# Spreading the keys of a banded attention over heads: by SBUF-to-SBUF DMAs instead of masked copies

## What is computed

```python
x = jnp.transpose(mask, (0, 2, 1))                 # the 256 columns are the positions, the 64 rows the features
q, k, v = jnp.split(x @ w_in.T + b_in, 3, axis=-1) # 8 heads of 8 features each
scores = jnp.einsum('bqhd,bkhd->bhqk', q, k) / jnp.sqrt(d)
band = jnp.abs(idx[:, None] - idx[None, :]) <= 64
scores = jnp.where(band[None, None], scores, neg)
attn = jax.nn.softmax(scores, axis=-1)
o = jnp.einsum('bhqk,bkhd->bqhd', attn, v).reshape(n, t, e)
```

## Time and profile before

| | us |
|---|---|
| median of 3 runs | 362.23 |
| lowest, highest | 362.06, 362.73 |
| profiled execution | 362.1 |
| its span, first to last instruction | 360.4 |

### The profile page before, as it was taken

How to read it: one execution, slowest core, us unless ns; L and a number is a source line. 1 busy time by engine, 2 the same in 40 slices (tenths; PEclk the granted TensorE clock), 3 DMA queues, 4 the chain that set the end, 5 groups by cost and what they waited for, 6 DMA issues and landing times.

```text
span 360.4 us, 7398 instructions
## 1 busy us (share of the span) xinstructions
PE 320.2 (89%) x2258; PEld 252.3 (70%) x2258; DVE 256.2 (71%) x935; ACT 208.1 (58%) x438; POOL 192.7 (53%) x287
## 2 busy tenths in 40 slices
PE   0689999779798898999999999899999999999993
PEld 0467768567576666767777777777777767888892
DVE  5899999999989899988323615576478846661364
ACT  2639888759687695967841341467577865213210
POOL 4757988758767585856602431515152543244733
PEclk9859999999999999999999999999999999999997
DMA  7996000000000000000000000000000000000011
GB/s 220 363 373 227 1 3 3 1 2 3 1 2 0 3 3 1 3 2 2 2 2 0 0 2 0 1 2 0 2 3 0 2 0 3 0 31 15 1 38 37
DMA packets 10150, 12.16 MB, mean 34 GB/s; under 512 B 1920, under 2 KB 8832, under 8 KB 10112
## 3 DMA queue, kind: packets, MB, share of 16 engines
q1 hardware_dynamic: 9536, 11.36, 9.2%
q10 hardware_dynamic: 576, 0.33, 0.4%
HBM read 10.64 MB, written 1.05 MB: 32 GB/s over the span
## 4 chain that ended last, share of the span: by engine, by line
PE 58%; DVE 27%; issue 8%; ACT 3%; POOL 2%; DMA 1%; POOLq 0%; DVEq 0%; SPq 0%; ACTq 0%
DVE masked L1110 10%; PE S L666 6%; PE S L339 5%; PE O L377 4%; PE ST L690 4%; PE S L472 4%; PE ST L361 4%; PE S L608 2%; PE S L536 2%; PE PJ L449 2%; PE PJ L579 2%; PE O L623 2%; PE PJ L310 2%; DVE st L1072 2%; PE XB L597 2%
## 5 line engine op out<-in xcount | busy, mean ns | idle before, releaser
L1110 DVE CUSTOM_DVE_ANT_0 masked<-S,band 128x192 bf16<-128x192 f32 x256 | 79.1, 353 | 8.4 <-PE S L339 7.3
L785 ACT ACTIVATE ex<-ST 128x384 f32<-128x384 f32 x128 | 62.2, 489 | 14.0 <-PE ST L361 13.4
L339 PE MATMUL S<-qk 128*128 128x384 f32 x128 | 53.5, 424 | 10.2 <-DVE mw L1110 8.1
L948 POOL TENSOR_SCALAR rstd<-mv 128x1 f32<-128x1 f32 x40 | 11.8, 294 | 94.2 <-DVE mv L1074 94.0
L960 POOL TENSOR_TENSOR qk<-kp,kmask 128x1024 fp32r<-128x1024 f32 x24 | 46.3, 1934 | 5.0 <-DVE kp L1208 4.9
L361 PE MATMUL ST<-qk 128*128 128x192 f32 x256 | 48.7, 273 | 0.0
L361 PEld LDWEIGHTS ST<-qk 128*128 128x128 f32 x256 | 44.5, 189 | 1.9 <-issue 1.2
L339 PEld LDWEIGHTS S<-qk 128*128 128x128 f32 x128 | 24.8, 195 | 23.3 <-issue 16.1
L1254 DVE TENSOR_REDUCE mw<-S 128x8 f32<-128x512 f32 x32 | 22.0, 687 | 17.9 <-PE S L536 17.8
L751 ACT ACTIVATE hs<-PJ,sb,cols 128x512 fp32r<-128x512 f32 x29 | 22.5, 777 | 20.6 <-PE PJ L311 20.1
L377 PE MATMUL O<-ex,v 128*32 128x192 f32 x512 | 34.2, 338 | 0.0
(11 more groups left out here) (178 smaller groups left out, 757.9 us busy)
## 6 DMA issues: line engine op xcount, KB each, us to landing
w<-in_w SPq DMA_DIRECT2D x2, 1024.0 KB, 10.1
cx<-in_cx SPq DMA_DIRECT2D x1, 1024.0 KB, 7.9
cxT<-in_cxT SPq DMA_DIRECT2D x1, 1024.0 KB, 9.6
up<-in_up SPq DMA_DIRECT2D x1, 1024.0 KB, 10.9
down<-in_down SPq DMA_DIRECT2D x1, 1024.0 KB, 11.8
out<-x SPq DMA_DIRECT2D x8, 128.0 KB, 1.7
x<-in_x SPq DMA_DIRECT2D x1, 768.0 KB, 5.6
vecs<-in_vecs SPq DMA_DIRECT2D x1, 640.0 KB, 8.0
```

The costliest lines, as they stand in the source:

```text
L339: mm(out, r32(qp[:, t % 2, g, b, P * c:P * c + P]), r32(mv_), start=True, stop=True).then_inc(s["pe_s"], 1)
L785: A(ex[:, (n // 2) % 4, 2 * w:2 * w + 2, :], ST[n % 2][:, 0:2 * WIN].rearrange("p (h k) -> p h k", h=2), ACT.Exp, scale=SCALE).then_inc(s[ ...
L1110: last = V.tensor_tensor_reduce(out=masked[:, n % 2, h, :], in0=S[n % 2][:, WIN * h:WIN * h + WIN], in1=band[:, c, :], scale=1.0, scalar=N ...
```

## The change

For tiles 2 and later both GpSimd's and ScalarE's masked copies are left out. SP issues, for each of those tiles, 24 DMAs from `kp` to `kb`: for each image b, each head j and each of the three blocks r, the eight rows of the head, both groups at once (8 partitions, 2 x 256 float32). They wait until both halves of the keys are written (`dve_mix`) and until the transposed scores of image b of the tile two before have been computed (`pe_st`). The other rows of a buffer keep what tiles 0 and 1 wrote. TensorE waits for the DMAs of its image (`ld_kb0`, `ld_kb1`), and VectorE waits for all 24 of the tile before, ahead of writing the keys of tile 3 and later.

```diff
         KA = {11: 0, 12: 1, 15: 2, 18: 3}
+        KB_DMA = 16 * 12
...
+            for t in range(2, TILES):
+                sp.wait_ge(s["dve_mix"], 4 * t + 2)
+                for b in range(2):
+                    sp.wait_ge(s["pe_st"], UNITS * (t - 2) + 8 * b + 8)
+                    for j in range(4):
+                        for r in range(3):
+                            rows = slice(32 * r + 8 * j, 32 * r + 8 * j + 8)
+                            sp.dma_start(kb[rows, t % 2, :, j, b, :], kp[rows, :, b, :]).then_inc(s[f"ld_kb{b}"], 16)
             ov = a["out"].rearrange("(t p) c -> p t c", p=P)
...
-                    if (b, g) == (1, 1):
+                    if t >= 2:
+                        pe.wait_ge(s[f"ld_kb{b}"], KB_DMA * (t - 1))
+                    elif (b, g) == (1, 1):
                         pe.wait_ge(s["act_kb"], t + 1)
...
-                    if j is not None and 0 <= t < TILES:
+                    if j is not None and 0 <= t < 2:
                         if j == 0:
                             act.wait_ge(s["dve_mix"], 4 * t + 2)
                             if t == 0:
                                 act.wait_ge(s["ld_small"], 64)
-                            if t >= 2:
-                                act.wait_ge(s["pe_st"], UNITS * (t - 1))
...
-                if t >= 2:
-                    pool.wait_ge(s["pe_st"], UNITS * (t - 2) + 8 * b + 4 * g + 4)
...
-                if l in KB and 0 <= t < TILES:
+                if l in KB and 0 <= t < 2:
                     keys(t, *KB[l])
...
-                    if n < 2 and t >= 1:
+                    if n < 2 and t in (1, 2):
                         dve.wait_ge(s["pool_kb"], 3 * t)
                         if g == 1:
                             dve.wait_ge(s["act_kb"], t)
+                    if n < 2 and t >= 3:
+                        dve.wait_ge(s["ld_kb0"], KB_DMA * (t - 2))
+                        dve.wait_ge(s["ld_kb1"], KB_DMA * (t - 2))
```

More of the change, by code:

```diff
@@ L147, in build @@
                  "dve_w dve_band dve_ln dve_xn dve_xl dve_mix dve_max dve_rc dve_on dve_x dve_zero "
-                 "pool_var pool_rstd pool_mw dve_y pool_kb pool_sel pool_zero act_kb dve_spread ld_sel "
+                 "pool_var pool_rstd pool_mw dve_y pool_kb pool_sel pool_zero act_kb ld_kb0 ld_kb1 dve_spread ld_sel "
                  "f_ln f_rstd f_xn f_sc f_cmp f_sel fp_sT fp_x fa_x fp_up fa_up fp_dn f_dn fp_sc f_x "
```

## The result

The changed kernel takes 382.38 us (median of 4 runs, 381.64 to 383.3), against 362.17 us before: ratio 1.0556, 95% interval 1.0524 to 1.0588. It is 5.6% slower, where I had forecast 355.4 us. The span is 379.9 us.

The account below looks back on a forecast made before the run. The prediction took VectorE, stalled under GpSimd's key copies, to bound most attention turns. From the 360.4 us span, - 7.3 us for stalls and + 0.5 us for new waits gave 353.6 us, so 355.4 us measured; range 352.5 to 366 us.

Parts of the forecast that it names:

- What bounds the kernel: Banded attention, turns from 59.7 us on: VectorE is the engine without a gap, standing still under 1.9 us GpSimd key copies.
- The gain, 7.3 us: VectorE in the banded attention: stalls under the 18 removed GpSimd copies, 8.3 us, less 1.0 us lost to selects.
- The 8.3 us of the earlier trace: Sum of VectorE's stalls at lines 1151, 1156 and 1169 under GpSimd key copies, in turns that VectorE bounds.
- The 1.0 us for selects in their place: VectorE instructions freed from copies sometimes start inside a GpSimd select: 9 stalls x 0.43 x 0.27 us given back.
- ScalarE's copies at 0: Removing 24 ScalarE copies, 12.2 us in all, gains nothing since no engine waited for them; at best 3 us.
- The interval of 0.47 us: SP's time from one DMA issue to the next, taken from back-to-back loads; bounds 0.37 and 0.73 us.
- The landing of 1.7 us: Time from a key DMA's issue to its landing, taken from the stores' median; the longest store took 3.2 us.
- The loop: SP's issue rate bounds each turn through VectorE's wait; slower than before from 0.58 us an issue; chance 0.17.
- The price at 0.65 us: If SP's issues are 0.65 us apart, a turn takes 22.35 us and the kernel 369.6 us.
- The new waits: VectorE's and TensorE's waits on the key DMAs are nearly always in time; 0.5 us of lateness, mostly tile 2.
- rival 2: GpSimd selects run earlier and stall the same VectorE instructions, and landings take 3.2 us: 361.0 us; chance 0.10.
- rival 3: SP's key DMAs don't overlap: 24 in a row take 40.8 us a tile, about 500 us in total; chance 0.03.

## Why the prediction was wrong

**What bounds the kernel**: right. VectorE's stalls under the copies were real and on the path; half of the DMAs, and the copies only moved, both show it.

**The gain, 7.3 us**: right in mechanism, low in size. It is 9.5 us. The 8.3 us of the earlier trace rows came back whole. The 1.0 us for selects in their place was an average over random starts, but the order is fixed, and the selects fell clear: line 1191's three stalls of 0.43 us went too.

**ScalarE's copies at 0**: right (362.82 us without them).

**The interval of 0.47 us**: this is the step that failed. It measured 0.73 us, the upper end that I had taken from one row behind full queues. I had argued that a small DMA on a quiet queue costs no more than a load, and by the earlier trace rows perhaps less. The rows I chose all had HBM on one side; none showed SBUF on both, and I said so and still took the ordinary value. Nothing in them bore on the form. Some other loads at the start took 1.2 to 5.6 us, so 0.73 us was not even the longest seen. With 0.73 us VectorE waited 1.9 to 3.4 us in each turn for the 24 DMAs that I had in time by 1.7 us, and my own sign of being wrong, an interval of 0.58 us or more, is what the trace shows.

**The landing of 1.7 us**: low by a little. It is 2.03 us from the start of the last issue, and 2.15 us to VectorE's start.

**The loop**: right as a rival. 23 i + 1.7 + 5.7 us with i = 0.728 gives 24.1 us a turn; with the measured landing (2.15) and second half (5.14) it is 24.0 us, and 24.06 us were measured in two of the five turns. That the first sum comes as near is in part luck, a landing too short and a second half too long. The mean is 24.5 us (122.4 / 5), with the long issues and the lower clock in it. My margin to the point of decision was 0.11 us of interval for a form the trace did not hold, and I gave it 0.17. The price at 0.65 us (369.6 us) was too low, since the interval went beyond it: the same sum at 0.728 us gives 379.3 us. Of the clock, which cost some 2 us more, the prediction says nothing.

**The new waits**: I put 0.5 us on them. They are two, and the experiment with the deeper source parts them: VectorE's wait on the source, 13 us, and TensorE's on the first 12, 7 us over before and 17 us over the version with half of the DMAs, the lower clock included.

**The other rivals**: the stalls did not move to the selects (rival 2), and the DMAs do overlap (rival 3): issues 0.73 us apart with landings of 2 us.

**A slip**: the first paragraph has 24 copies removed. The change removes 18 of the 24, and the stalls were summed for those 18.

## What to carry to other kernels

A queue that issues many small DMAs is an engine with a busy time: count its issues times the interval of exactly that form, and close the loop over the buffer that the DMAs read, before counting what they free. Where the trace lacks the form, measure it, or let the forecast hang on what the upper bound would do and not on the usual value. And before work is taken off an engine, look at what stands beside it: moving the copies by two slots gave 6 of the 9.5 us at no cost.

## What was not expected of the hardware

- An SP issue between two SBUF tiles took 0.59 to 0.69 us (medians) in all seven forms tried, one partition or 128. In the other small groups a load from HBM or a store to it took 0.29 to 0.47 us (medians), unless its 16 rows lay at one even distance in HBM and as eight partitions of two in SBUF: then 0.66 us. The two versions through HBM show the same, 0.649 against 0.299 us. Why an even distance, or SBUF on both sides, costs the sequencer more is not settled; no experiment looked inside an issue.
- A store of 384 KB took 3.0 us from its issue to its landing in HBM, an output store of 128 KB 1.7 us.
- TensorE's granted clock went from 1.00 to 0.50 of full speed (from 2.4 to 1.2 GHz) in each turn of the changed kernel from tile 4 on, in or soon after a stretch of 3.3 to 3.9 us in which TensorE stood idle for VectorE, and was back at 1.00 some 3.5 to 7 us later; over the turn from 137.5 to 162.5 us it is 0.84. In the version with half of the DMAs, without such a stretch, it stayed at 1.00 in those turns.
